# Late gathers with landing places of their own, and a copy on ScalarE

## The chip, the cores and the metric

The kernel runs on one core of one Trainium2 chip. The metric is the device time of one execution in microseconds. TensorE (PE), VectorE (DVE), ScalarE (ACT), GpSimd (POOL) and SyncE (SP) each run an instruction stream of their own and wait for one another through semaphores. SP, ACT and POOL can start DMA transfers.

## The reference

A graph has 6,250 nodes with 64 features each (x), and 200,000 edges sorted by destination, each with a source, a destination, a weight and 64 attributes. Five graph operators are computed and mixed:

```
deg_w = max(segment_sum(w, dst), 1);  deg_c = max(segment_sum(1, dst), 1)
xs    = x[src]
gcn   = segment_sum(w / sqrt(deg_w[src] * deg_w[dst]) * xs) @ Wgcn + b
sage  = x @ Wsage_s + segment_sum(xs) / deg_c @ Wsage_n + b
gin   = ((1 + eps) * x + segment_sum(w * xs)) @ Wgin + b
gconv = x @ Wgc1 + segment_sum(w * xs) @ Wgc2 + b
eop   = segment_sum(w * relu(xs + edge_attr)) @ Wedge + b
out   = layernorm(x + sum of the five, each times its weight)
```

All of it is float32. What costs time is xs = x[src], 200,000 rows of 64 numbers, and the five segment sums.

## The kernel before, in words

The edges are cut into 196 chunks of 1,024 (128 partitions by TILES = 8). A chunk's edges have destinations in a window of at most 40 nodes, so its segment sums are a matrix product: `segment_sums` (L1261) multiplies, for each of the 8 tiles, 128 feature columns (64 of relu(xs + attr), 64 of xs) with 120 columns of one-hot windows (plain, times w, times w and the source's root). Float32 matmuls stand in the profile as two each, so a chunk's product is 16 matmuls of 120 columns. VectorE adds the product to the running sums (`add_sums`, L1065).

The rows of x reach a chunk in three ways:

- 16 **early** chunks: POOL gathers their rows of x at the start (L526), and a chain of ScalarE (L661), TensorE (L1312) and VectorE (L1089 to L1103) finds their root weights.
- 20 **picked** chunks: without DMA. ScalarE makes one-hot nodes (`hot_nodes`, L688 and L691), TensorE multiplies them with the table in SBUF (`pick_tile`, L1280, 14 matmuls of 455 columns per tile of 128 edges), and VectorE picks the row (`pick`, L988 and L992).
- 160 **late** chunks: POOL gathers rows of 68 numbers (64 of x, the inverse root of the degree, padding) from the table `node_table` in DRAM, with 8 indirect DMAs of 128 rows for each chunk (L559).

A late chunk goes round a ring of UNROLL = 4 places, u = 0 to 3. In order of the data:

- ScalarE copies the indices of two chunks, for the next round, into `idx` (L653, semaphore `staged`), when it comes to its own chunk with odd u and the gathers of this pair have landed.
- POOL waits for `staged` and for `chunk_product`, the product of the chunk four before, and gathers into columns D to BLOCK of `feat[:, u]`, the tile that this product reads (L556 to L559).
- VectorE (`features`) waits for `chunk_product`, makes the windows (L1070), waits for the gather, multiplies the root weights (L950) and adds the rows to the attributes (L953, semaphore `summed_in`), which SP has loaded (L421).
- ScalarE (`late_chunk`, L650 to L655) waits for `summed_in` and writes the relu beside the rows (semaphore `relu_ready`).
- VectorE weights the windows (`weigh_hots`, L1076); TensorE (`late_chunk`) waits for relu, windows and the sums of four chunks before, and makes the product.

The stages: a start (degrees, table) with the early gathers; a node stage (L1223, L1228 on TensorE, L627, L635 on ScalarE), during which the first four late chunks are gathered, since `chunk_product` got its start value of 4 when TensorE began; an **early stage** of 4 rounds, in which each late chunk goes with an early one; a **turn stage** of 35 rounds, in which each late chunk goes with one pick tile (two in every seventh) and two half chunks of picked edges go with each seven; one plain round; the end. Every engine runs its instructions in the order written; each loop body is one turn of 28 late chunks. `relu_ready` and its like get their start values on ScalarE behind the node stage (L639). ScalarE's `hot_nodes` stands ahead of its late chunk in four of seven slots.

`window` (L834 to L839) computes the windows of all edges by way of `scratch`, once per pass; there is one pass here.

Of the kernel before, what the change touches and what calls it, by code (L numbers as in the profile page):

```python
# [28 lines left out]
ALU = mybir.AluOpType  # L29
# [56 lines left out]
def build(nc, x, src, dst, edge_attr, edge_weight, mix, Wgcn, bgcn, Wsage_s, Wsage_n, bsage,  # L86
          gin_eps, Wgin, bgin, Wgc1, Wgc2, bgc, Wedge, bedge, out):
    ctx = ExitStack()
    with ctx:
# [26 lines left out]
        row_w = area[:, 4 * CHUNK:6 * CHUNK].rearrange("p (g e) -> p g e", g=2)  # L116

        attr = sb("attr", [P, UNROLL, TILES, D])
        FEATS, HOTS = UNROLL * TILES * BLOCK, UNROLL * TILES * 3 * WINDOW
        ring = sb("ring", [P, FEATS + HOTS])  # L120
        feat = ring[:, 0:FEATS].rearrange("p (u j b) -> p u j b", u=UNROLL, b=BLOCK)

        hot = ring[:, FEATS:FEATS + HOTS].rearrange("p (u j k n) -> p u j k n", u=UNROLL, k=3, n=WINDOW)
        attr_flat = attr[:, :, :, :].rearrange("p u j b -> p (u j b)")
# [13 lines left out]
        e_win = sb("e_win", [P, CHUNKS, TILES], BF16)  # L138

        scratch = sb("scratch", [P, CHUNKS * TILES])  # L140
        e_tmp = scratch[:, :].rearrange("p (c j) -> p c j", j=TILES)
        e_w = sb("e_w", [P, CHUNKS, TILES])

# [158 lines left out]
        hots_ready = sem("hots_ready")  # L302
        summed_in = sem("summed_in")
        relu_ready = sem("relu_ready")
        chunk_product = sem("chunk_product")
        early_idx_loaded, early_gathered = sem("early_idx_loaded"), sem("early_gathered")

# [195 lines left out]
        @block.gpsimd  # L503
        def _(pool):
            nc.gpsimd.memset(ident[:], 0.0).then_inc(pool_chain, 1)
            nc.gpsimd.memset(row_far[:], 0.0).then_inc(pool_chain, 1)
            nc.gpsimd.memset(ones[:], 1.0).then_inc(consts, 1)
            pool.wait_ge(pool_chain, 2)
            nc.gpsimd.affine_select(out=ident[:], in_=ident[:], compare_op=ALU.not_equal, fill=1.0, base=0,
                                    pattern=[[-1, P]], channel_multiplier=1).then_inc(consts, 1)  # L510

            nc.gpsimd.affine_select(out=row_far[:, 0:LAST_OLD], in_=row_far[:, 0:LAST_OLD], compare_op=ALU.not_equal,
                                    fill=FAR, base=-(HIGH - 1), pattern=[[0, LAST_OLD]],
                                    channel_multiplier=1).then_inc(far_ready, 1)
            nc.gpsimd.iota(iota_b[:], [[1, NT]], base=0, channel_multiplier=0,
                           allow_small_or_imprecise_dtypes=True).then_inc(consts, 1)
            nc.gpsimd.iota(minus_ids[:], [[-1, SPLIT]], base=0, channel_multiplier=-SPLIT,
                           allow_small_or_imprecise_dtypes=True).then_inc(consts, 1)
            for t, step, n in ((slots, 1, WINDOW), (cuts, 1, WINDOW + 1), (row_starts, NT, P + 2)):
                nc.gpsimd.iota(t, [[step, n]], base=0, channel_multiplier=0,  # L520
                               allow_small_or_imprecise_dtypes=True).then_inc(consts, 1)

            pool.wait_ge(early_idx_loaded, 16)
            def gather_early(c):
                for j in range(TILES):
                    nc.gpsimd.indirect_dma_start(  # L526
                        out=early_x[:, c, j], out_offset=None, in_=x,
                        in_offset=bass.IndirectOffsetOnAxis(ap=early_idx[:, c, j:j + 1], axis=0),
                    ).then_inc(early_gathered, 16)

            for c in range(HEAD):
                gather_early(c)
                if c == 0:
                    nc.gpsimd.iota(root_part[:, NT:NT + 1], [[0, 1]], base=0, channel_multiplier=1,
                                   allow_small_or_imprecise_dtypes=True).then_inc(consts, 1)
                    nc.gpsimd.iota(minus_mid[:], [[0, 1]], base=-(NT // 2), channel_multiplier=-NT,
                                   allow_small_or_imprecise_dtypes=True).then_inc(consts, 1)

                    nc.gpsimd.memset(table_sb[:, :, D:TROW], 0.0).then_inc(pad_x, 1)
                    nc.gpsimd.memset(table_sb[:, N % NT:, 0:D], 0.0).then_inc(pad_x, 1)  # L540

            pool.wait_ge(base_stored, 1)
            n_pass = pool.value_load(passes[0:1, 0:1], min_val=1, max_val=WINDOWS)
            with pool.Fori(0, n_pass) as v:
                pool.wait_ge(product_g, v * UNITS + 2)
                pool.sem_inc(gathers_begun, 1)
                for c in range(HEAD, EARLY):
                    if c > PACED:
                        pool.wait_ge(weight_done, 2 * (c - PACED) - 1)
                    gather_early(c)  # L550
                pool.wait_ge(table_stored, 16)
                with pool.Fori(0, LATE_STEPS) as i:
                    for u in range(UNROLL):
                        it = v * LATE + i * UNROLL + u
                        pool.wait_ge(staged, v * (LATE // 2) + i * (UNROLL // 2) + u // 2 + 1)
                        pool.wait_ge(chunk_product, it + 1)  # L556
                        pool.sem_inc(gathers_begun, 1)
                        for j in range(TILES):
                            nc.gpsimd.indirect_dma_start(  # L559
                                out=feat[:, u, j, D:BLOCK], out_offset=None, in_=table,  # L560
                                in_offset=bass.IndirectOffsetOnAxis(ap=idx[:, u, j:j + 1], axis=0),
                            ).then_inc(gathered[u], 16)

        @block.scalar
        def _(act):
# [71 lines left out]
                    lift_x(k + 2)  # L637

            act.sem_inc(relu_ready, UNROLL)  # L639
            act.sem_inc(early_relu_ready, 1)  # L640
            act.sem_inc(distance_ready, 1)
            act.sem_inc(relu_g, 2)
# [3 lines left out]
            with act.Fori(0, n_pass) as v:  # L646
                act.wait_ge(early_gathered, early_landed(v))

                def late_chunk(i, u):
                    if u % 2:  # L650
                        act.wait_ge(gathered[u - 1], (v * LATE_STEPS + i + 1) * (16 * TILES))
                        act.wait_ge(gathered[u], (v * LATE_STEPS + i + 1) * (16 * TILES))
                        nc.scalar.copy(idx[:, u - 1:u + 1], e_src[:, bass.ds((i + 1) * UNROLL + u - 1 + BASE, 2)]).then_inc(staged, 1)  # L653
                    act.wait_ge(summed_in, v * LATE + i * UNROLL + u + 1)
                    nc.scalar.activation(feat[:, u, :, 0:D], attr[:, u], ACT.Relu).then_inc(relu_ready, 1)  # L655

                def far_sources(c):
# [82 lines left out]
        def _(dve):  # L740
# [192 lines left out]
            link(nc.vector.memset(win_off[:], 0.0))  # L933
            with dve.Fori(0, n_pass) as v:
                dve.wait_ge(early_gathered, early_landed(v))
                window(v, 0)
                nc.vector.tensor_copy(w_late[:, UNROLL - 1], e_w[:, BASE])

                def features(i, u, last=False):
# [4 lines left out]
                    if u == 1:  # L944
# [2 lines left out]
                        nc.vector.tensor_copy(w_late[:, 0:n], e_w[:, bass.ds(c, n)])  # L947
                    window_hots(hot[:, u], e_win[:, c])
                    dve.wait_ge(gathered[u], turn * (16 * TILES))
                    nc.vector.tensor_tensor(out=wroot[:, u], in0=e_w[:, c], in1=feat[:, u, :, 2 * D], op=ALU.mult)  # L950
                    loaded = (v * (LATE_STEPS + 1) if u > 1 else v * LATE_STEPS) + i + 1
                    dve.wait_ge(attr_loaded[u // 2], (loaded + (u > 1 and last)) * 16)
                    nc.vector.tensor_tensor(out=attr[:, u], in0=attr[:, u], in1=feat[:, u, :, D:2 * D],  # L953
                                            op=ALU.add).then_inc(summed_in, 1)

                def weigh_hots(i, u):
# [409 lines left out]
```

## Time and profile before

| | |
|---|---|
| three runs | 2224.48, 2230.78, 2244.31 us, median 2230.78 |
| the profiled execution | 2228.75 us, its span 2226.9 us |
| TensorE matmul, weight load | 1556.4 us (70%), 1007.5 us (45%) |
| VectorE | 928.6 us (42%) |
| ScalarE | 826.9 us (37%) |
| POOL | 1355.2 us (61%) |
| late gathers, L559 | 1280 instructions, 1228.4 us |
| mean granted TensorE clock | 0.867 of full speed |

Busy time is that of instructions in execution. A matmul's end is modelled. Waits are the idle time of an engine ahead of an instruction, put down to what ended last by the profile; "remote" means that no recorded event explains the end of a wait, "issue" that the engine waited for nothing the profile shows.

### The profile page before, as it was taken

The numbers are of one execution on the slowest core, as the hardware profiler recorded it, in microseconds if no ns is written. First come the engines' busy times: TensorE is split into PE (matmuls) and PEld (weight loads), VectorE is DVE, ScalarE is ACT, GpSimd is POOL, SyncE is SP. The second block draws the span as 40 slices with busy tenths as digits, with TensorE's granted clock in tenths as the row PEclk, the third lists the DMA queues.
The fourth block names the chain that finished last, engine by engine and source line by source line (L and its number), as shares of the span: only waits on it lengthen the run. The fifth ranks groups of instructions, "written<-read, shape, count | busy, mean of one in ns | idle before, by whom it ended". The sixth has DMA issues, their size and how long they took to land.

```text
span 2226.9 us, 22565 instructions
## 1 busy us (share of the span) xinstructions
PE 1556.4 (70%) x6037; PEld 1007.5 (45%) x6037; DVE 928.6 (42%) x2539; ACT 826.9 (37%) x1201; POOL 1355.2 (61%) x1426
## 2 busy tenths in 40 slices
PE   1004367566888777877878778777887888877876
PEld 1003367553554544544445445444444445544546
DVE  5684256543433332433433433243333334423346
ACT  1676233243433433424244234233333324423323
POOL 7665366556666656656666666566666656665660
PEclk9999967688989888978889888888888888888988
DMA  5111234331222222222222222222222222222223
GB/s 98 23 24 51 70 100 112 95 80 42 51 64 45 55 54 46 57 46 44 54 57 53 47 57 43 47 58 50 48 66 43 48 51 57 47 53 44 59 55 77
DMA packets 83186, 126.12 MB, mean 57 GB/s; under 512 B 29494, under 2 KB 31269, under 8 KB 82821
## 3 DMA queue, kind: packets, MB, share of 16 engines
q0 software_dynamic: 45056, 48.85, 13.6%
q1 hardware_dynamic: 36371, 74.90, 11.0%
q10 hardware_dynamic: 1650, 1.04, 0.2%
q8 instruction: 53, 0.87, 0.2%
q14 instruction: 56, 0.46, 0.1%
HBM read 121.29 MB, written 3.40 MB: 56 GB/s over the span
## 4 chain that ended last, share of the span: by engine, by line
PE 43%; issue 18%; another core or an unknown queue 17%; DVE 10%; ACT 4%; POOL 3%; DVEq 2%; DMA 1%; SPq 0%; POOLq 0%; ACTq 0%
PE psum L1280 27%; PE psum L1261 13%; ACT ring L604 4%; POOL ring L559 3%; DVE ring L1076 2%; DVE sums L1065 2%; DVE early L988 1%; PE psum L1312 1%; PE psum L1228 1%; DVE attr L953 1%; DVE early L992 1%; DMA ring<-node_table,idx 1%; PE psum L1341 1%; PE psum L1342 1%
## 5 line engine op out<-in xcount | busy, mean ns | idle before, releaser
L559 POOL DMA_INDIRECT ring<-node_table,idx x1280 | 1228.4, 960 | 758.2 <-issue 389.4
L1280 PE MATMUL psum<-table_sb,early_x 128*128 128x455 f32 x2240 | 988.1, 586 | 115.6 <-issue 110.1
L1280 PEld LDWEIGHTS psum<-table_sb,early_x 128*128 128x128 f32 x2240 | 446.0, 205 | 573.4 <-issue 566.7
L1261 PE MATMUL psum<-ring 128*128 128x120 f32 x2560 | 405.3, 313 | 246.5 <-issue 127.5
L1261 PEld LDWEIGHTS psum<-ring 128*128 128x128 f32 x2560 | 375.5, 224 | 310.2 <-issue 164.9
L988 DVE TENSOR_TENSOR early<-psum,digit_hot 128x455 f32<-128x455 f32 x160 | 100.6, 631 | 989.5 <-remote 599.3
L688 ACT ACTIVATE early_x<-early,minus_ids 128x256 f32<-128x256 f16 x560 | 370.4, 744 | 138.7 <-remote 103.4
L655 ACT ACTIVATE ring<-attr 128x512 f32<-128x512 f32 x160 | 100.2, 626 | 483.4 <-DVE attr L953 383.8
L679 ACT ACTIVATE early<-early 128x256 f32<-128x256 f32 x40 | 16.7, 416 | 518.2 <-DVE early L1009 385.1
L1065 DVE TENSOR_TENSOR sums<-sums,psum 64x40 f32 (+1 forms) x648 | 127.5, 197 | 97.4 <-remote 53.6
L526 POOL DMA_INDIRECT early_x<-in_x,early_idx x128 | 122.0, 953 | 61.4 <-issue 40.3
L1261 PE MATMUL psum<-early 128*128 128x120 f32 x576 | 102.7, 340 | 77.8 <-issue 53.7
L1076 DVE TENSOR_TENSOR ring<-ring,psum 128x320 f32<-128x320 f32 x320 | 141.6, 484 | 6.0 <-issue 1.0
L691 ACT ACTIVATE early_x<-early_x,ones 128x1792 f32<-128x1792 f32 x80 | 143.1, 1788 | 2.6
L1261 PEld LDWEIGHTS psum<-early 128*128 128x128 f32 x576 | 98.0, 251 | 98.5 <-issue 72.7
L953 DVE TENSOR_TENSOR attr<-attr,ring 128x512 f32<-128x512 f32 x160 | 109.6, 685 | 0.0
L877 DVE SCALAR_TENSOR_TENSOR early<-attr,scratch,psum 128x1024 bf16<-128x1024 f32 x80 | 98.1, 1275 | 24.2 <-issue 22.6
L992 DVE TENSOR_REDUCE early<-early 128x65 f32<-128x455 f32 x160 | 98.5, 627 | 4.2
L1236 PE MATMUL psum<-ring 128*128 128x98 f32 (+1 forms) x8 | 2.0, 435 | 137.8 <-DVE ring L894 137.8
L604 ACT ACTIVATE ring<-attr,scratch 128x1024 bf16<-128x1024 f32 x82 | 93.0, 1137 | 10.6 <-issue 10.4
L1070 DVE TENSOR_TENSOR ring<-e_win,psum 128x320 f32<-128x320 f32 (+1 forms) x160 | 77.1, 482 | 18.2 <-issue 11.4
L1236 PEld LDWEIGHTS psum<-ring 128*128 128x128 f32 (+1 forms) x8 | 1.8, 327 | 138.0 <-DVE ring L894 138.0
(158 smaller groups left out, 644.8 us busy)
## 6 DMA issues: line engine op xcount, KB each, us to landing
attr<-in_edge_attr SPq DMA_DIRECT2D x79, 512.0 KB
ring<-node_table,idx POOLq DMA_INDIRECT x1280
early<-in_edge_attr SPq DMA_DIRECT2D x36, 256.0 KB
src_all<-in_src SPq DMA_DIRECT2D x16, 512.0 KB
early<-key_rows SPq DMA_DIRECT2D x10, 512.0 KB
early_x<-degree_rows SPq DMA_DIRECT2D x2, 1568.0 KB
early_x<-in_x,early_idx POOLq DMA_INDIRECT x128
node_table<-table_sb SPq DMA_DIRECT2D x1, 1666.0 KB, 6.0
```

The source lines that it names most:

```text
L526: nc.gpsimd.indirect_dma_start(out=early_x[:, c, j], out_offset=None, in_=x, in_offset=bass.IndirectOffsetOnAxis(ap=early_idx[:, c, j:j + ...
L559: nc.gpsimd.indirect_dma_start(out=feat[:, u, j, D:BLOCK], out_offset=None, in_=table, in_offset=bass.IndirectOffsetOnAxis(ap=idx[:, u, j: ...
L604: last = nc.scalar.activation(signs[0:rows, k % TURNS], row_dst[0:rows, g], ACT.Sign, bias=cuts[0:rows, n:n + 1], scale=-1.0, accum_out=si ...
L688: last = nc.scalar.activation(to[:, :, a], keys[:, tile:tile + 2], ACT.Square, bias=minus_ids[:, a:a + 1])
L691: nc.scalar.activation(to, to, ACT.Relu, bias=ones[:, 0:1], scale=-2.0).then_inc(node_hot_made, 1)
L953: nc.vector.tensor_tensor(out=attr[:, u], in0=attr[:, u], in1=feat[:, u, :, D:2 * D], op=ALU.add).then_inc(summed_in, 1)
L988: nc.vector.tensor_tensor(out=picks[:, k % 2], in0=pick_ps[k % 2].rearrange("p (b c) -> p c b", b=SPLIT), in1=hot_c, op=ALU.mult).then_inc ...
L992: last = nc.vector.tensor_reduce(out=feat_g[:, half, k, D:2 * D + 1], in_=picks[:, k % 2], axis=AX.X, op=ALU.add)
L1065: last = nc.vector.tensor_tensor(out=sums[of, k, to], in0=sums[of, k, to], in1=acc[ps, part * WINDOW:(part + 1) * WINDOW], op=ALU.add)
L1076: return nc.vector.tensor_tensor(out=to[:, :, k], in0=to[:, :, 0], in1=by.unsqueeze(2).to_broadcast([P, n, WINDOW]), op=ALU.mult)
L1261: last = nc.tensor.matmul(to[:, 0:3 * WINDOW], features[:, j, 0:2 * D], hots[:, j].rearrange("p k n -> p (k n)"), start=(j == 0), stop=(j ...
L1280: last = nc.tensor.matmul(pick_ps[k % 2].rearrange("p (b c) -> p b c", b=SPLIT), node_hot[:, k, a], table_sb[:, a * SPLIT:(a + 1) * SPLIT, ...
```

## The change

Late gathers land in four places of their own, `landing`, two of them new and two inside `scratch`. ScalarE copies the 64 features of a landed chunk into the product's tile and increments `lifted`. POOL waits for `lifted` of the chunk four before, not for its product. `lifted` gets its start value of 4 on ScalarE behind the node stage. The product's tile has 128 columns in place of 132. VectorE reads rows and root weight from the landing place. Since two places lie in `scratch`, VectorE's `window` waits for the lifts of the pass before, and POOL waits for `windows_set` ahead of the third chunk of each round (u = 2).

```diff
-        FEATS, HOTS = UNROLL * TILES * BLOCK, UNROLL * TILES * 3 * WINDOW
+        FEATS, HOTS = UNROLL * TILES * 2 * D, UNROLL * TILES * 3 * WINDOW
...
-        feat = ring[:, 0:FEATS].rearrange("p (u j b) -> p u j b", u=UNROLL, b=BLOCK)
+        feat = ring[:, 0:FEATS].rearrange("p (u j b) -> p u j b", u=UNROLL, b=2 * D)
...
+        landing_free = sb("landing", [P, UNROLL // 2, TILES, TROW])
+        landing = [landing_free[:, k] for k in range(UNROLL // 2)] + [
+            scratch[:, k * TILES * TROW:(k + 1) * TILES * TROW].rearrange("p (j b) -> p j b", b=TROW) for k in range(UNROLL - UNROLL // 2)]
...
+        lifted = sem("lifted")
...
 (POOL)
-                        pool.wait_ge(chunk_product, it + 1)
+                        pool.wait_ge(lifted, it + 1)
+                        if u == UNROLL // 2:
+                            pool.wait_ge(windows_set, v + 1)
                         pool.sem_inc(gathers_begun, 1)
                         for j in range(TILES):
                             nc.gpsimd.indirect_dma_start(
-                                out=feat[:, u, j, D:BLOCK], out_offset=None, in_=table,
+                                out=landing[u][:, j], out_offset=None, in_=table,
...
 (ScalarE, behind the node stage)
             act.sem_inc(relu_ready, UNROLL)
+            act.sem_inc(lifted, UNROLL)
...
 (ScalarE, late_chunk)
                     act.wait_ge(summed_in, v * LATE + i * UNROLL + u + 1)
+                    nc.scalar.copy(feat[:, u, :, D:2 * D], landing[u][:, :, 0:D]).then_inc(lifted, 1)
                     nc.scalar.activation(feat[:, u, :, 0:D], attr[:, u], ACT.Relu).then_inc(relu_ready, 1)
...
 (VectorE, ahead of window)
                 dve.wait_ge(early_gathered, early_landed(v))
+                dve.wait_ge(lifted, v * LATE + UNROLL)
...
 (VectorE, features)
-                    nc.vector.tensor_tensor(out=wroot[:, u], in0=e_w[:, c], in1=feat[:, u, :, 2 * D], op=ALU.mult)
+                    nc.vector.tensor_tensor(out=wroot[:, u], in0=e_w[:, c], in1=landing[u][:, :, D], op=ALU.mult)
...
-                    nc.vector.tensor_tensor(out=attr[:, u], in0=attr[:, u], in1=feat[:, u, :, D:2 * D],
+                    nc.vector.tensor_tensor(out=attr[:, u], in0=attr[:, u], in1=landing[u][:, :, 0:D],
```

## Rows read from the trace of the kernel before

**Rows 1.** Page: engines' busy time and share, then the chain by engine.
```profile
PE 1556.4 (70%) x6037; PEld 1007.5 (45%) x6037; DVE 928.6 (42%) x2539; ACT 826.9 (37%) x1201; POOL 1355.2 (61%) x1426
...
PE 43%; issue 18%; another core or an unknown queue 17%; DVE 10%; ACT 4%; POOL 3%; DVEq 2%; DMA 1%; SPq 0%; POOLq 0%; ACTq 0%
```
**Rows 2.** Line L559's instructions: what they waited for, who waited for them.
```profile
  remote: 215.8, 69
  ACT idx L653: 117.4, 18
  PE psum L1261: 35.6, 13
...
  ACT idx L653: 8.3, 1
  DVE psum L950: 5.5, 1
```
**Rows 3.** Timeline: start, duration, instruction, [idle before <- releaser], of three engines.
```profile
1666.39 0.63 ACT L655 ACTIVATE ring<-attr 128x512 f32<-128x512 f32 x1 [2.25 <-DVE attr L953]
...
1677.73 0.94 POOL L559 DMA_INDIRECT ring<-node_table,idx  x1 [2.26 <-remote]
1714.64 1.08 POOL L559 DMA_INDIRECT ring<-node_table,idx  x1 [6.70 <-ACT idx L653]
...
1714.22 0.68 DVE L953 TENSOR_TENSOR attr<-attr,ring 128x512 f32<-128x512 f32 x1
```
**Rows 4.** Windows: start:end, length, busy PE, PEld, DVE, ACT, POOL, clock, DMA share, GB/s.
```profile
718.80:733.80 15.00, 15.00 (x56) 9.37 (x56) 9.78 (x31) 8.02 (x12) 11.32 (x12) 0.91 0.27 67
733.80:740.60 6.80, 1.40 (x8) 0.99 (x6) 0.00 (x0) 0.00 (x0) 3.78 (x4) 0.86 0.23 51
...
780.90:797.90 17.00, 4.79 (x23) 3.56 (x22) 0.00 (x0) 0.00 (x0) 11.44 (x13) 0.66 0.20 35
...
1692.70:1709.70 17.00, 8.96 (x14) 2.83 (x15) 0.00 (x0) 0.00 (x0) 11.58 (x13) 0.75 0.18 27
1714.60:1729.60 15.00, 13.19 (x56) 9.66 (x57) 8.43 (x26) 10.67 (x15) 10.49 (x11) 0.76 0.27 59
```
**Rows 5.** Windows over the node stage.
```profile
197.00:217.00 20.00, 19.55 (x94) 18.02 (x94) 3.65 (x8) 6.53 (x14) 9.43 (x10) 1.00 0.32 104
217.00:232.00 15.00, 3.12 (x14) 2.30 (x12) 0.00 (x0) 0.70 (x2) 11.32 (x12) 1.00 0.19 28
...
247.00:257.00 10.00, 6.93 (x34) 6.37 (x32) 1.00 (x3) 3.15 (x9) 0.00 (x0) 1.00 0.00 0
```
**Rows 6.** POOL's timeline in the early stage.
```profile
285.89 0.94 POOL L559 DMA_INDIRECT ring<-node_table,idx  x1 [2.46 <-remote]
```
**Rows 7.** Windows: the early and the turn stage.
```profile
265.00:480.00 215.00, 139.16 (x786) 134.29 (x787) 125.78 (x361) 72.48 (x88) 125.26 (x128) 0.71 0.38 104
480.00:2140.00 1660.00, 1313.50 (x4693) 784.54 (x4691) 606.88 (x1775) 593.99 (x861) 1049.78 (x1096) 0.87 0.23 51
```
**Rows 8.** POOL's timeline in the turn stage: two bursts begin.
```profile
718.82 0.94 POOL L559 DMA_INDIRECT ring<-node_table,idx  x1 [3.51 <-remote]
...
742.34 0.94 POOL L559 DMA_INDIRECT ring<-node_table,idx  x1 [3.85 <-remote]
```
**Rows 9.** ScalarE's timeline: the node stage's copies, the first relu.
```profile
201.76 0.37 ACT L635 COPY parts_h<-psum 128x256 f32<-128x256 f32 x1 [1.33 <-PE psum L1228]
...
211.57 0.37 ACT L635 COPY parts_h<-psum 128x256 f32<-128x256 f32 x1 [1.02 <-PE psum L1228]
...
256.93 0.64 ACT L635 COPY parts_h<-psum 128x256 f32<-128x256 f32 x2 [1.29 <-PE psum L1228]
...
266.31 0.63 ACT L655 ACTIVATE ring<-attr 128x512 f32<-128x512 f32 x1 [1.84 <-DVE attr L953]
```
**Rows 10.** ScalarE's nearest copy; TensorE's wait for the windows (us, times, longest).
```profile
L670 ACT COPY early<-early_x 128x512 f32 x12 | 7.4, 615 | 23.2 <-issue 10.4 <-PE psum L1261 9.5 <-remote 3.3
...
PE psum L1261 <- DVE ring L1076: 105.3, 32, 7.3
```

## The prediction

> **What bounds the kernel now.** I began with the page's totals [rows 1]. TensorE is busy for 70% of the span, POOL 61%, VectorE 42%, ScalarE 37%, and the chain is 43% TensorE with 18% "issue" and 17% "unknown". A third of the chain is time that no engine owns, so the question is who makes TensorE slow.
>
> Second, the waits around the late gathers [rows 2]. POOL pauses before 100 of its gathers: 69 times "remote" (215.8 us) and 13 times on TensorE's product (35.6 us), 18 times on the copy of indices (117.4 us). The code has only two waits in front of a chunk, `staged` and `chunk_product`, so "remote" is a product whose end the profile doesn't show. 160 chunks over 100 pauses are 1.6 chunks in one uninterrupted burst. The same answer says who waits for a gather to land: 8.3 us once, 5.5 us once, in the whole run. Rows that landed lie there: the gathers that begin at 1677.73 have all been issued 10 us later, and VectorE adds them at 1714.22 [rows 3]. **Gathers are early already**; starting them earlier has 14 us to win, at most.
>
> Third, stretches of single bursts [rows 4], the view on which all rests. I cut five bursts into their first 15 us and what is left of them with some 3 us beyond. In the first 15 us TensorE retires 56 matmuls in the first and 56 in the last of the five, 284 in 75 us in all: 3.8 a us. In the rest it retires 8 in 6.8 us, 10 in 6.6 us (not shown), 23 in 17 us and 14 in 17 us: 55 in 47.4 us, 1.16 a us, and neither VectorE nor ScalarE runs anything. After the next pause it is at full rate again. Call this the crawl.
>
> Is it the gathers? Two other places say so. In the node stage gathers 0 to 3 run without a pause for 40 us [rows 5]: TensorE retires 94 matmuls in the 20 us to 217, then 14 in 15 us, and 34 in the 10 us after the burst, in straight-line code with other operands. And in the early stage POOL runs single chunks (16 in 215 us, 13.4 us each [rows 7]) with pauses like the 2.46 us of [rows 6]: no crawl there. The granted clock doesn't explain it: in the node stage it is 1.00 throughout, in the crawls of rows 4 it is 0.86, 0.66 and 0.75, while the rate falls to a third. By "TensorE: Matmul & The Clock Gate" (The HAM clock gate) of the Trainium skill the array is either at 2.4 or at 1.2 GHz, which could halve the rate and no more; the trace goes beyond it, so the cause must lie elsewhere. The page also reports a clock stuck at a quarter, which would be rival A below.
>
> So POOL and TensorE regulate each other: a long burst makes TensorE crawl, its product comes late, **the product's wait stops POOL, and the stop frees TensorE**.
>
> **The law in numbers.** A burst of n chunks lasts 10n us (12 gathers in 15 us [rows 4], 8 to a chunk). TensorE is at full rate from 3 us after its end to 15 us into the next: p + 12 us, with p the pause. It crawls for 10n − 12 us. A chunk needs 4693 / 137 = 34.3 matmuls (1096 gathers are 137 chunks [rows 7]). So 34.3n = 3.8(p + 12) + 1.16(10n − 12), p = (22.7n − 31.7) / 3.8.
> - n = 2: p = 3.6, 23.6 us, 11.8 a chunk. The trace: bursts of two begin at 718.82 and 742.34 [rows 8], 23.5 apart; the whole stage 1660 / 137 = 12.1.
> - n = 3: p = 9.6, 13.2 a chunk. n = 4: p = 15.6, 13.9 a chunk.
> - n = 1 has no crawl; POOL's 10 us and a pause rule.
>
> **The change, part by part.**
> 1. *The wait on the product becomes a wait on the lift.* ScalarE lifts chunk m before its relu, which precedes the product; the product has a pick tile before it, and in a crawl its own matmuls too. Of the two waits only `staged` and the lift are left. Of 100 pauses the 82 of "remote" and product lose their cause. Rows 3 show one: the gathers of chunk 119 wait 2.26 us for a product, up to 1677.73, though chunk 115's relu was at 1666.39; with the lift they follow at once, and bursts of one and three chunks become one of four. What ends a burst then is the index copy, for which POOL waited 6.70 us up to 1714.64; it is made when ScalarE gets to its odd chunk, which needs VectorE, which needs the pick tiles. I take n = 3, between today's 1.6 and the four places: (13.2 − 12.1) × 137 = **+151 us**. Bounds: n = 2, 11.8 a chunk, −41 us (nothing to +0 if today's mean stays); n = 4, +247 us.
> 2. *The first four chunks.* `lifted` gets its start value on ScalarE behind the node stage, `chunk_product` got it at TensorE's start. So gathers 0 to 3 leave the node stage, and its crawl goes. Copies L635 came every 2.45 us (201.76 to 211.57); the 13th would come at 201.76 + 12 × 2.45 = 231.2 and came at 256.93 [rows 9]: **−26 us**.
> 3. *The same gathers land on the early stage.* The first begins at about 231.5 and its chunk has landed at about 243.5 (10 us of issue and an estimated 2 to land); chunk 0's relu, at 266.31 now [rows 9], would be due at 240.3 and comes at about 244.3: +4 us. POOL goes on through chunk 5, 60 us: 48 us of crawl give 56 matmuls; a chunk of this stage takes 786 / 16 = 49, so 1.1 chunks instead of 48 / 13.4 = 3.6: 2.5 × 13.4 = +33 us. The other ten, in bursts of two: 98 = 3.95(p + 12) + 1.16 × 8 (3.95: 786 in 199 us of work), p = 10.5, 15.2 a chunk against 13.4 [rows 7]: +18 us. Together **+55 us**; bounds 0 (the bursts stay single) and +90.
> 4. *The lift's own cost.* 160 copies of 128x512. Nearest row: L670, the same shape, 615 ns [rows 10]: 98 us on an engine that is idle 63% of the time. On the path it lies where TensorE waits for a relu or hots at the head of a product: 32 waits on L1076 [rows 10] and a few on L655. There the hots end beside the relu, so half of 0.62 × 35 = 22 counts: **+10 us**, bounds 0 and +22. Queued behind it on ScalarE are the relu, the node hots (L688) for the next tiles, and the staging copy.
> 5. *Nothing:* VectorE reads the rows and the root weight from the landing place instead of the block, same shapes. `windows_set` is awaited before the third chunk; the window is two VectorE instructions of 128x1568, about 2 us each as three times L953's 0.68 [rows 3], and two chunks (20 us) of gathers cover it; without that cover it would cost POOL these 4 us, once. VectorE's new wait for the lift's start value moves the window by no more than the first relu's wait for rows (item 3) hides. SP's queue has no new step. The product reads blocks of 128 floats, not 132: no row prices it; 0, bounds ±5.
>
> The sum is made against the profiled execution's own 2228.75 us (span 2226.9), 2 us under the median of 2230.78: 2228.75 + 151 − 26 + 55 + 10 = 2419, with 2 us to the median 2421. I say **2420 us**.
>
> **Rivals.**
> - *A: the crawl is TensorE's own (a clock held low), not the gathers'.* Then landed rows are not awaited anyway, the node stage keeps its crawl, and only the lift is added: 2231 + 10 = 2240. For it: the granted clock does dip in the turn stage. Against it: the node stage at clock 1.00 and the ends of crawls, each within 3 us of a burst's end.
> - *B: POOL's waits are the bound.* The usual rule, "double-buffer for performance" (Trainium Kernel Development and Optimization, Best Practices, in the Trainium skill), would have it so; rows 2 disagree, with 14 us of waiting for landed rows. If the 251 us of pauses for products went and TensorE kept its 3.8 a us (34.3 matmuls in 9.0 us), POOL's 10 us a chunk would pace it: 2231 − 251 + 10 = 1990; with half of that gain 2110. It decides if a burst of three no longer brings a crawl.
> - *C: the staging copies alone hold bursts at two.* Item 1 is 0 instead of +151, item 3 half: 2231 − 26 + 27 + 10 = 2242.
> - *D: as C, and the early stage stays single and the lift is hidden:* 2231 − 26 = 2205.
> - *E: the change doesn't bring gathers forward* because `staged` always comes last: that is C or D in its times.
>
> **Chances.** Forecast 0.64 (2280 to 2600), A 0.07, B 0.14, C with E 0.10, D 0.05. One per cent (22 us) is about what a measurement of this kernel can tell from no change; the three runs lie within 0.9%. Faster by over 1%: B and D, 0.19. Within 1%: A and C, 0.17. Slower: 0.64. The range leaves out B and the uppermost bursts of four: 2200 to 2520; the forecast's own is 2300 to 2520.
>
> **What would show it.** POOL's pauses fall from 100 to 40 to 60, those left mostly on L653. Windows set as in rows 4, from 15 us into a burst to its end, hold about 1.2 matmuls a us and make up over 40% of the turn stage. The first late gather starts near 231 and the last L635 near 231. L655 stands behind an equal copy of 0.62 us. The time between bursts of three is about 40 us. I am wrong if TensorE goes on at 3.8 a us past the 20th us of a burst, or if most pauses stay.

## The result and the profile after

| | before | after |
|---|---|---|
| runs, us | 2224.48 to 2244.31, median 2230.31 (4) | 2482.02 to 2509.45, median 2498.45 (4) |
| the profiled execution, its span | 2228.75, 2226.9 | 2509.45, 2507.6 |
| TensorE's mean granted clock | 0.867 | 0.798 |

The ratio is 1.119, 95% interval 1.112 to 1.126: 268 us slower at the median, where 190 were forecast. 2498 lies inside the range of 2200 to 2520, near its upper end. The profiled execution of after is the slowest of its four, so its stages add up to 281 us and not 268.

The page's totals of after, engines and then the chain, answer to [rows 1]. The matmuls are as many as before; ScalarE has 160 instructions more.

```profile
PE 1626.3 (65%) x6037; PEld 1006.5 (40%) x6037; DVE 927.0 (37%) x2539; ACT 910.8 (36%) x1361; POOL 1349.4 (54%) x1426
...
PE 45%; issue 24%; another core or an unknown queue 15%; DVE 11%; ACT 1%; DVEq 1%; DMA 1%; POOL 1%; SPq 0%; ACTq 0%; POOLq 0%
```

The late gathers of after (L565), what they waited for and who waited for their landing, answer to [rows 2]. The product is gone from the list. POOL waits for the lift (L662) 32 times and for the index copy (L660) 28 times, 601 us together, where its waits were 369 us before ("issue" left out in both). Hardly anybody waits for landed rows, as before: 14.8 us in the whole run.

```profile
  ACT ring L662: 391.3, 32
  ACT idx L660: 210.0, 28
...
  DVE psum L959: 8.6, 2
  ACT idx L660: 6.2, 1
```

Windows over one burst of four chunks in the turn stage of after, then over the start of the next burst of three and its rest, answer to [rows 4] (start:end, length, busy PE, PEld, DVE, ACT, POOL with counts, clock, DMA share, GB/s). TensorE retires 64 matmuls in the first 15 us and 13 in the 28 us after them, up to 3 us past the burst's end; then 61 and 9.

```profile
965.40:980.40 15.00, 13.39 (x64) 8.79 (x64) 7.97 (x23) 11.22 (x17) 11.65 (x12) 1.00 0.25 62
980.40:1008.40 28.00, 9.63 (x13) 3.07 (x12) 1.27 (x4) 4.92 (x8) 18.90 (x20) 0.59 0.22 45
1028.30:1043.30 15.00, 12.18 (x61) 8.03 (x59) 4.42 (x13) 7.67 (x12) 11.34 (x13) 1.00 0.25 62
1043.30:1061.00 17.70, 7.92 (x9) 2.30 (x8) 1.40 (x3) 0.00 (x0) 11.31 (x12) 0.51 0.14 26
```

POOL's timeline, the first gathers of these two bursts. The second one waited 22.91 us for the lift of a chunk whose rows had landed long before. All four places were full, because TensorE had got through only 13 matmuls while they were being filled; during this pause it catches up.

```profile
965.37 1.29 POOL L565 DMA_INDIRECT landing<-node_table,idx  x1 [4.79 <-ACT idx L660]
...
1028.30 0.94 POOL L565 DMA_INDIRECT landing<-node_table,idx  x1 [22.91 <-ACT ring L662]
```

TensorE inside the crawl: two matmuls, each with the weight load behind it (L1289 is the pick tile; the lines of PE's and PEld's timelines are put together in order of time). A matmul of this tile starts every 0.38 us at full rate (14 of them take 5.52 us from 1015.70) and every 2.1 to 2.9 us here, and the starts of these four stand 0.70, 1.40 and 0.70 us apart. The time before each is "issue", which is no wait for another engine that the profile shows.

```profile
992.62 0.92 PE L1289 MATMUL psum<-table_sb,early_x 128*128 128x455 f32 x1 [1.92 <-issue]
993.32 0.29 PEld L1289 LDWEIGHTS psum<-table_sb,early_x 128*128 128x128 f32 x1 [1.80 <-issue]
...
994.72 0.92 PE L1289 MATMUL psum<-table_sb,early_x 128*128 128x455 f32 x1 [1.18 <-issue]
995.42 0.29 PEld L1289 LDWEIGHTS psum<-table_sb,early_x 128*128 128x128 f32 x1 [1.81 <-issue]
```

The node stage of after, windows, then ScalarE's timeline with its last copy and the first relu, answer to [rows 5] and [rows 9]. The stage keeps its 4.7 to 4.9 matmuls a us to the end, and the gathers begin behind it (at 228.42).

```profile
197.00:217.00 20.00, 20.00 (x98) 18.60 (x97) 2.94 (x6) 8.19 (x17) 0.00 (x0) 1.00 0.22 89
217.00:228.00 11.00, 10.47 (x52) 9.95 (x51) 0.63 (x3) 3.97 (x10) 0.00 (x0) 1.00 0.01 1
```
```profile
227.08 0.64 ACT L641 COPY parts_h<-psum 128x256 f32<-128x256 f32 x2 [1.29 <-PE psum L1237]
...
241.60 0.62 ACT L663 ACTIVATE ring<-attr 128x512 f32<-128x512 f32 x1
```

**Where the time went.** I cut both executions at the relus of late chunks 0, 16 and 156. Up to the first: 266.3 before, 241.6 after, −24.7. The sixteen chunks of the early stage: 208.7 and 281.2, +72.4. The 140 chunks up to number 156: 1681.4 and 1923.4, 12.0 and 13.7 us each, +242.0. The end: 70.4 and 61.4, −9.0, which no item of the forecast has and no run explains. The sum is 280.7, the difference of the spans (all differences are of unrounded times). Counted as matmuls of one product or pick tile that stand more than 1.15 us apart, joined to stretches, TensorE crawls for some 320 us before, in 56 stretches, and for some 790 us after, in 51: about as many stretches, nearly three times as long. (How they are joined matters: the gaps inside the tiles alone make 311 and 672 us.)

A second count needs no threshold for a slow matmul. Take of each burst in those 140 chunks what lies behind its first 15 us. Before, these pieces make 398 us (24%) with 1.8 matmuls a us; after, 617 us (32%) with 0.76. Outside them TensorE retires 3.2 and 3.3 a us, in 1284 and 1307 us. So 219 of the 242 us lie in the long ends of bursts.

### The profile page after: what moved, and what is told of

Its sections match the earlier page's. It is cut to its first block, busy times and chain, and to the rows that moved or that the text cites. A ratio compares the mean times of both kernels' runs of the same rounds, so it can differ in the third digit from the quotient of the medians.

```text
span 2507.6 us, 22767 instructions
## 1 busy us (share of the span) xinstructions
PE 1626.3 (65%) x6037; PEld 1006.5 (40%) x6037; DVE 927.0 (37%) x2539; ACT 910.8 (36%) x1361; POOL 1349.4 (54%) x1426
## 4 chain that ended last, share of the span: by engine, by line
PE 45%; issue 24%; another core or an unknown queue 15%; DVE 11%; ACT 1%; DVEq 1%; DMA 1%; POOL 1%; SPq 0%; ACTq 0%; POOLq 0%
PE psum L1289 30%; PE psum L1270 12%; DVE early L885 3%; DVE ring L1085 1%; PE psum L1321 1%; DVE sums L1074 1%; DVE early L997 1%; PE psum L1237 1%; ACT early_x L696 1%; DVE attr L962 1%; POOL landing L565 1%; PE psum L1350 0%; PE psum L1351 0%; PE psum L1232 0%
## 5 line engine op out<-in xcount | busy, mean ns | idle before, releaser
L1289 PE MATMUL psum<-table_sb,early_x 128*128 128x455 f32 x2240 | 1072.6, 615 | 297.9 <-issue 297.3
L565 POOL DMA_INDIRECT landing<-node_table,idx x640 | 612.4, 957 | 550.6 <-ACT ring L662 227.4
L565 POOL DMA_INDIRECT scratch<-node_table,idx x640 | 610.3, 954 | 492.0 <-issue 204.6
L1289 PEld LDWEIGHTS psum<-table_sb,early_x 128*128 128x128 f32 x2240 | 460.6, 211 | 826.9 <-issue 826.3
L1270 PE MATMUL psum<-ring 128*128 128x120 f32 x2560 | 396.3, 301 | 285.2 <-issue 194.4
L1270 PEld LDWEIGHTS psum<-ring 128*128 128x128 f32 x2560 | 361.5, 214 | 352.3 <-issue 253.9
L662 ACT COPY ring<-scratch 128x512 f32<-128x512 f32 x80 | 49.1, 614 | 480.5 <-DVE attr L962 423.9
L662 ACT COPY ring<-landing 128x512 f32<-128x512 f32 x80 | 49.1, 613 | 271.8 <-DVE attr L962 217.5
L1270 PE MATMUL psum<-early 128*128 128x120 f32 x576 | 94.4, 325 | 44.8 <-issue 22.1
L1270 PEld LDWEIGHTS psum<-early 128*128 128x128 f32 x576 | 91.4, 238 | 64.7 <-issue 39.9
## 6 DMA issues: line engine op xcount, KB each, us to landing
early_x<-degree_rows SPq DMA_DIRECT2D x2, 1568.0 KB, 13.7
```

Source lines behind the costliest of these rows:

```text
L565: nc.gpsimd.indirect_dma_start(out=landing[u][:, j], out_offset=None, in_=table, in_offset=bass.IndirectOffsetOnAxis(ap=idx[:, u, j:j + 1] ...
L1270: last = nc.tensor.matmul(to[:, 0:3 * WINDOW], features[:, j, 0:2 * D], hots[:, j].rearrange("p k n -> p (k n)"), start=(j == 0), stop=(j ...
L1289: last = nc.tensor.matmul(pick_ps[k % 2].rearrange("p (b c) -> p b c", b=SPLIT), node_hot[:, k, a], table_sb[:, a * SPLIT:(a + 1) * SPLIT, ...
```

## The experiments

Each was timed beside the kernel before on the same chip. That kernel takes 2205 us on the first of the three chips used, 2229 on the second, so ratios are compared (the changed kernel's is 1.119). Unless said otherwise an experiment is the changed kernel with one edit.

**Was it the freed gathers, or the lift?** `product_wait` puts the old wait back and leaves all else.

```diff
                         pool.wait_ge(lifted, it + 1)
+                        pool.wait_ge(chunk_product, it + 1)
```

> The changed kernel with the old wait on chunk_product put back ahead of each late chunk, beside the wait on the lift: the lift, its copies, the landing places and the later start stay, the freedom of the gathers goes. Crawl theory: bursts go back to those of the kernel before, 2231 - 30 (node stage) + 20 (first gathers on the early stage) + 10 (lift) = 2230 us, range 2210 to 2270. Rival 'the lift and the new tiles cost the time': stays near 2500.

2207.84 us against 2205.22: ratio 1.004 (1.001 to 1.008). The loss is gone with one wait, though the lift, its 160 copies and the landing places are all still there.

`late_start` is the kernel before with only the later start:

```diff
                 pool.wait_ge(table_stored, 16)
+                pool.wait_ge(relu_ready, UNROLL)
```

> The kernel before, only POOL waits for the end of ScalarE's node stage ahead of the first late gather. Crawl theory: node stage -30 (no gathers beside it), the first four chunks then run unpaused beside the early stage, +20: 2220 us, range 2200 to 2240. What product_wait takes beyond this is the lift's own cost, expected 10 us, 0 to 22. Rival 'the node stage is slow of itself': no -30, 2250 or more.

2208.95 us, ratio 1.001 (0.996 to 1.005). In its profile the node stage ends 32 us earlier (last copy at 225.4, before 257.4), and chunk 16's relu comes at 483.3 where it came at 475.0: the gathers' crawl is paid once, beside the one stage or the other. Against product_wait this leaves −1 us for the lift. Each of the two was run ten times and spreads over 33 us, so this can't be told from some 10 us either way.

**Do pauses end the crawl?** `pause8` and `pause16` make POOL wait for the landing of its own last gather.

```diff
                             ).then_inc(gathered[u], 16)
+                            if j == TILES - 1:               # pause16: and u % 2 == 1
+                                pool.wait_ge(gathered[u], (v * LATE_STEPS + i) * (16 * TILES) + 16 * (j + 1))
```

> The changed kernel, and POOL waits after each late chunk for the landing of its own last gather before it issues the next chunk. Crawl theory (gathers issued without a pause for some 15 us make TensorE crawl, a pause of 2 to 3 us ends it): bursts are 10 us, no crawl, POOL's 9.7 + 2.9 = 12.6 us a chunk rules: turn stage 137 x 12.6 = 1726 against 1660 before (+66), node stage -30, early stage 16 x 12.6 = 202 against 215 (-13): about 2255 us, 240 us faster than the changed kernel although POOL does the same work and waits more. Rival 'TensorE's own clock': nothing changes, about 2500. Rival 'it is the lift or the new tiles that cost': nothing changes or slower by the added waits, 2500 or more.

> The changed kernel, and POOL waits for the landing of its last gather after every second late chunk. Crawl theory: bursts of 20 us with some 5 us of crawl and a pause of 2.9: 22.3 us for two chunks if TensorE gets its 68.6 matmuls in: 3.8 x 17.3 + 1.16 x 5 = 71.5, just enough: 11.2 to 11.6 us a chunk, turn stage 1530 to 1590, sum 2070 to 2150 us: faster than both kernels. If the crawl's rate is 0.5 a us and its onset at 13 us, TensorE falls behind and bursts stretch as before, about 2200. Rival 'TensorE's own clock': 2500.

2287.25 us (ratio 1.038, 1.030 to 1.045) and 2400.37 (1.091, 1.083 to 1.099). With a pause behind each chunk there is no stretch of crawl in the whole run, and the kernel with more waits takes 7% less time than the changed one, by the ratios. POOL's timeline in pause8, the first gathers of two chunks, and the windows over these two chunks: the chunk before ended 2.4 us earlier, the chunks begin 12.2 us apart, and TensorE retires 32 and 44 matmuls. That pace, 12.4 us in the mean, is what the kernel now takes.

```profile
705.39 0.94 POOL L565 DMA_INDIRECT landing<-node_table,idx  x1 [2.42 <-DMA landing<-node_table,idx]
...
717.60 0.95 POOL L565 DMA_INDIRECT scratch<-node_table,idx  x1 [2.52 <-ACT idx L662]
```
```profile
705.40:717.60 12.20, 10.70 (x32) 7.08 (x33) 3.97 (x13) 7.79 (x12) 7.55 (x8) 0.72 0.15 24
717.60:729.80 12.20, 12.16 (x44) 6.58 (x42) 5.79 (x18) 1.40 (x3) 7.57 (x8) 1.00 0.34 87
```

With a pause behind each second chunk TensorE crawls for some 490 us in 76 stretches. The 2070 to 2150 expected for it were wrong: 20 us of gathers with 2.6 us behind them still bring the crawl. `pause13` (the loop goes over two rounds, with a pause behind every 13th gather) asks where the limit is:

> The changed kernel, and POOL waits for the landing of its last gather after every 13th (five pauses in 64 gathers), ahead of the point where the crawl sets in. Crawl theory: (80 + 5 x 2.6) / 8 = 11.6 us a chunk, little crawl: 240 + 205 + 140 x 11.6 + 65 = 2135 us, up to 2200: between 0 and 3% faster than the kernel before, and 5% faster than pause8 and pause16. If the onset were a matter of chunks or of POOL's loop and not of gathers in a row, it would lie between pause8 and pause16, 2287 to 2400.

2302.74 us, 1.032 (1.028 to 1.036): a miss, against 2135 to 2200. It crawls in 60 stretches, some 335 us. Of the 44 bursts of 12 gathers and more in its turn stage that begin behind a pause under 2.5 us (mostly 2.3), 26 retire only 13 to 30 matmuls of products and picks in their first 15 us. Of the 26 behind a longer pause one does; the others retire 41 to 66. So a pause of 2.3 us often does not undo 16 us of gathers, while 2.4 us undo 10. The expectation's other branch, an onset set by chunks or by POOL's loop, named a place between pause8 and pause16; the ratio is no higher than pause8's 1.038, which speaks against it, but the intervals overlap. No setting of pauses tried beats the kernel before.

**What in the gathers is it?** `narrow` fetches 16 bytes for each late row in place of 272, so its output is not the right one; `landing_free` is cleared once at the start:

```diff
-                                out=landing[u][:, j], out_offset=None, in_=table,
+                                out=landing[u][:, j, 0:4], out_offset=None, in_=table.rearrange("n (k w) -> (n k) w", w=4),
```

> The changed kernel, whose late gathers fetch pieces of 4 numbers (16 bytes) in place of rows of 68 (272 bytes), as many descriptors and as many gathers (the numbers fetched are others). If bytes moved by the gathers cause the crawl, it shrinks or goes: 2000 to 2250 us. If the issue of gathers or the descriptors cause it, nothing changes: 2450 to 2520 us.

2493.21 us, 1.119 (1.110 to 1.129): the changed kernel's time with a seventeenth of the bytes in a late row, and with a seventh of all the bytes of the gathers' queue, early gathers included (its line in narrow's page, then in after's: packets, MB, share).

```profile
q0 software_dynamic: 45056, 6.91, 4.6%
```
```profile
q0 software_dynamic: 45056, 48.85, 11.2%
```

Windows over a burst in narrow show 68 matmuls in 15 us and 11 in the 26 us after them.

```profile
762.30:777.30 15.00, 14.51 (x68) 9.22 (x66) 7.57 (x21) 10.23 (x15) 11.34 (x13) 1.00 0.15 35
777.30:803.70 26.40, 9.25 (x11) 3.06 (x11) 0.00 (x0) 3.26 (x5) 17.87 (x19) 0.59 0.11 21
```

`memset7` keeps POOL busy with an eighth of the DMAs. Seven of eight rows are zeros in it, so its output is not the right one either; the waits of ScalarE and VectorE for landed rows are fitted to one gather and the memsets (not shown):

```diff
-                        for j in range(TILES):
-                            nc.gpsimd.indirect_dma_start(...).then_inc(gathered[u], 16)
+                        nc.gpsimd.indirect_dma_start(...)        # j = 0 alone
+                        for j in range(2 * (TILES - 1)):
+                            nc.gpsimd.memset(landing[u][:, 1:TILES], 0.0).then_inc(filler, 1)
+                            pool.wait_ge(filler, it * (2 * (TILES - 1)) + j + 1)
```

> The changed kernel, in which seven of the eight gathers of each late chunk are left out: in their place POOL runs 14 memsets of 128x476 on the landing place, about as long as the gathers were (seven eighths of the rows are zeros). POOL stays as busy, only the indirect DMAs are gone. If the gathers themselves make TensorE crawl: no crawl, POOL's 10 us a chunk or TensorE's 9.0 rules, 240 + 180 + 140 x 10.3 + 65 = 1930 us, up to 2050. If any unbroken work of POOL's makes it crawl: about 2500. If it is TensorE's own clock: about 2500 too.

2042.95 us, 0.917 (0.915 to 0.920), and no stretch of crawl. POOL's timeline, the end of one chunk and the gather of the next; then windows over two chunks, which take 10.9 and 11.0 us.

```profile
607.04 0.49 POOL L571 MEMSET landing<- 128x476 f32 x1 [0.15 <-POOL landing L571]
607.69 0.49 POOL L571 MEMSET landing<- 128x476 f32 x1 [0.15 <-POOL landing L571]
609.28 0.95 POOL L566 DMA_INDIRECT scratch<-node_table,idx  x1 [1.10 <-issue]
```
```profile
554.10:565.00 10.90, 9.47 (x28) 6.43 (x29) 3.85 (x12) 7.60 (x12) 7.90 (x15) 0.69 0.18 51
565.00:576.00 11.00, 11.00 (x47) 6.81 (x46) 3.74 (x11) 7.61 (x11) 7.91 (x16) 1.00 0.15 53
```

`busy_pause` puts five memsets of 128x544 ahead of each chunk's gathers, each waited for:

```diff
+                        for k in range(5):
+                            nc.gpsimd.memset(landing[u], 0.0).then_inc(filler, 1)
+                            pool.wait_ge(filler, it * 5 + k + 1)
...
                         for j in range(TILES):
```

> The changed kernel, with five memsets of 128x544 by POOL (about 3 us) ahead of the gathers of each late chunk: a pause in the gathers, but none in POOL's work. If a pause in the gathers is enough to end the crawl: no crawl, 9.7 + 3.2 = 12.9 us a chunk, 240 + 206 + 140 x 12.9 + 65 = 2320 us. If POOL has to stand still: crawls as in the changed kernel and POOL's extra 3 us a chunk, 2500 to 2700 us.

2519.78 us, 1.131 (1.128 to 1.135). The time alone looks like a failure of the theory that a pause ends the crawl; the profile says the opposite. There is no stretch of crawl: TensorE retires 33 and 41 matmuls in two chunks of 14 us each. POOL's timeline shows 4.2 us between the gathers, not 3.2, and a chunk takes 14.0 us, by POOL alone:

```profile
611.24 0.94 POOL L571 DMA_INDIRECT scratch<-node_table,idx  x1 [0.30 <-issue]
612.18 0.57 POOL L567 MEMSET scratch<- 128x544 f32 x1
...
616.36 0.95 POOL L571 DMA_INDIRECT scratch<-node_table,idx  x1 [0.79 <-POOL scratch L567]
```
```profile
573.00:587.00 14.00, 7.83 (x33) 4.63 (x32) 6.83 (x22) 2.30 (x5) 10.46 (x13) 0.89 0.31 76
587.00:601.00 14.00, 10.22 (x41) 7.26 (x41) 3.87 (x12) 6.92 (x10) 10.43 (x14) 0.87 0.13 20
```

So the crawl stays away though POOL itself works on; only the price for the memsets was 1 us too low. What pause8 and busy_pause don't tell is whether it is the pause that does it, or the slower pace of gathers that comes with it.

**Is it the pace, or the pause?** `spaced4` and `spaced3` put a memset of one column behind every second (about every third) gather. POOL waits for them only once, ahead of the next chunk:

```diff
+                        pool.wait_ge(filler, it * 4)         # spaced3: it * 3
...
+                            if j in (1, 3, 5, 7):            # spaced3: (2, 4, 7)
+                                nc.gpsimd.memset(spare[:, u * TILES + j:u * TILES + j + 1], 0.0).then_inc(filler, 1)
```

> The changed kernel with a one-column memset on POOL behind every second gather, so that the gathers come at 1.55 us each on average (12.4 us a chunk) and never pause for more than about 1.1 us. Pace theory (the crawl comes when gathers run at more than about one per 1.5 us for some 15 us: pause8 had 1.51 us each and no crawl, pause13 1.42 us each and crawls): no crawl, 240 + 205 + 140 x 12.4 + 65 = 2245 us, like pause8. Pause theory (only 2 us and more without a gather end or prevent it): crawls in long stretches, 2500 us or more.

> The same with three memsets a chunk: 1.48 us a gather, 11.8 us a chunk. Pace theory: at the edge; without crawl 240 + 195 + 140 x 11.8 + 65 = 2150 us, 3% faster than the kernel before; with some crawl, as pause13, 2200 to 2300. Pause theory: 2500.

2503.44 us, 1.134 (1.124 to 1.143), and 2485.93, 1.128 (1.120 to 1.136). They don't tell: the memset fell into the 0.30 us that stood between two gathers anyway, so the pace hardly changed, and TensorE crawls for about 600 us in both. POOL's timeline in spaced4:

```profile
908.01 0.94 POOL L569 DMA_INDIRECT landing<-node_table,idx  x1 [0.30 <-issue]
908.94 0.13 POOL L574 MEMSET spare<- 128x1 bf16 x1
909.26 0.95 POOL L569 DMA_INDIRECT landing<-node_table,idx  x1 [0.19 <-issue]
```

`waited4` and `waited3` have a wait behind each memset instead (`pool.wait_ge(filler, ...)`), which keeps the next gather back:

> As spaced4, whose memsets fell into the 0.30 us between two gathers and left them 1.28 us apart, but POOL now waits for each memset before it issues the next gather: by the 0.79 to 1.10 us seen between a waited-for memset and a gather in the two kernels with memsets, 1.55 to 1.7 us a gather, 12.5 to 13.7 us a chunk, no gap above 1.3 us. Pace theory: no crawl, 240 + 210 + 140 x 13 + 65 = 2335 us (2265 to 2435). Pause theory (only about 2 us and more without a gather prevent it): crawls as in spaced4 (500 us and more of them), 2500 us or more.

> The same with three waited-for memsets a chunk: 1.48 to 1.6 us a gather, 11.9 to 12.8 us a chunk. Pace theory: little crawl (pause8 had none at 1.51 us a gather in the mean, pause13 some at 1.42), 240 + 195 + 140 x 12.3 + 65 = 2220 us (2165 to 2300). Pause theory: 2480 us, as spaced3.

2298.44 and 2203.02 us, no crawl in either. That reads like the pace theory, but they ran on the third chip, and the kernel before shows that they prove nothing: **the kernel before took 1831.39 us there** (7 runs, 1829.96 to 1835.66), so the ratios are 1.254 (1.251 to 1.258) and 1.203 (1.200 to 1.205). Nothing in the two traces of this chip crawls. The clearest place is code that none of these kernels touches, at the start, beside the early gathers. VectorE's timeline in the kernel before (a chain of small dependent steps), then in waited4:

```profile
45.69 0.16 DVE L868 SCALAR_TENSOR_TENSOR ring<-ring 128x2 f32<-128x2 f32 x1 [1.23 <-DVE ring L867]
46.39 0.17 DVE L867 TENSOR_SCALAR ring<-ring 128x2 f32<-128x2 f32 x1 [0.54 <-issue]
47.79 0.20 DVE L868 SCALAR_TENSOR_TENSOR ring<-ring 128x2 f32<-128x2 f32 x1 [1.23 <-issue]
```
```profile
38.05 0.16 DVE L883 SCALAR_TENSOR_TENSOR ring<-ring 128x2 f32<-128x2 f32 x1
38.24 0.17 DVE L882 TENSOR_SCALAR ring<-ring 128x2 f32<-128x2 f32 x1
38.45 0.16 DVE L883 SCALAR_TENSOR_TENSOR ring<-ring 128x2 f32<-128x2 f32 x1
```

Windows over the same stretch, before and then waited4: POOL's gathers are as many and stand 1.25 us apart in both, but VectorE and ScalarE are busy for twice and five times as long.

```profile
30.00:60.00 30.00, 3.77 (x20) 2.80 (x18) 14.32 (x47) 5.24 (x6) 22.97 (x24) 1.00 0.26 34
```
```profile
30.00:60.00 30.00, 3.38 (x16) 2.61 (x16) 27.23 (x65) 28.46 (x49) 22.99 (x24) 1.00 0.19 30
```

It is the chip and not the kernel: in this stretch VectorE is busy for 8.8 to 17.3 us in every one of the twelve traces from the other chips, and for 27.2 in both from the third. There is no profile of the kernel before on that chip, and the changed kernel was not run on it; that its 1831 us are 2205 without the crawl is likely and not shown. Whether the change would gain there, as rival B has it, is open, and so is pace against pause on a chip that crawls.

## Why the prediction was right, and where its sizes were off

**The bound.** Right: TensorE's slow stretches beside unbroken gathers. Rival A (TensorE's own clock) is out: pause8 and busy_pause make the stretches vanish by edits of POOL's stream alone, memset7 by taking gathers away, and the slow steps of VectorE above stand in a window whose granted clock is 1.00. Inside after's two crawls shown above the granted clock is 0.59 and 0.51, in the 15 us before each 1.00; the rate falls from 4.3 and 4.1 matmuls a us to 0.5, and half a clock doesn't give an eighth of the rate. The clock records of both traces hold full speed and half of it, and no quarter. Late loading of code, a rival that the prediction doesn't name, doesn't explain the first of these crawls: from 978 to 1020 us no packet of a queue of kind "instruction" moves in after. Rival B (POOL's waits are the bound) is out on the chips that crawl. On the third chip the prediction's law fails, since it gives the kernel before some 2230 us there and 1831 were measured. Rivals C, D and E fell with the turn stage's +242, E also with the 32 waits for the lift.

**Item 1, the turn stage, +151, measured +242.** The sign and the mechanism hold, two sizes did not. The prediction took bursts of three throughout; counting pauses of 1.95 us and more, after has 67 bursts (2.4 chunks each; 88 of 1.8 before): 19 of one chunk, 16 of two, 22 of three, 10 of four and more. By the law that alone would have made the term smaller. The other size is the crawl's rate, 1.16 matmuls a us from four stretches. In after the rest of a burst, up to 3 us past its end, holds 7 to 13 matmuls in 20 of the 22 bursts of three (18 us) and 11 to 23 in the eight of four (28 us): more length brings few more matmuls, and the mean is 0.75 a us. With 10 in place of 1.16 (10n − 12), the law reads p = (34.3n − 10) / 3.8 − 12: 11.7 us a chunk for n = 2, 14.1 for n = 3, 15.4 for n = 4. The measured 13.7 lies between.

That repair is not shown, for neither law holds length by length. From one burst's start to the next, in the turn stage of after, a chunk takes 15.5 us in bursts of one, 14.1 in bursts of two, 12.5 in bursts of three and 15.2 in bursts of four. In the kernel before, seven bursts of three took 12.1 us a chunk, where the law gives 13.2, and bursts of two took 12.1 as well. The prediction tested its law at n = 2 only; these seven bursts were there to test it at n = 3. So the balance within one burst gave the direction; for the size no law is shown. That the term came within a factor of two is in part luck: a burst length too long stood against a rate too high.

**What ends a burst.** The prediction said the index copy. After has 32 waits for the lift (391 us), with all four places full, and 28 for the copy (210 us). In the prediction's count (100 before) these are 60 pauses, at the edge of its 40 to 60; by length, 66 are of 1.95 us and more (87 before) and 76 of 0.5 and more (106 before). Of its other signs, the rest of the bursts, from 15 us on, makes 32% of the turn stage, not over 40, at 0.76 matmuls a us and not 1.2; bursts of three begin 37.6 us before the next burst, not 40; the first gather comes at 228.4 and the last node copy at 227.5 for its 231.

**Items 2 and 3.** Node stage −26: measured −24.7 to the first relu, −30 to the last copies. (The copy at 256.93 is the twelfth and not the thirteenth, which came at 257.35; so counted the item would have been −28 or −26.) Early stage +55: measured +72.4. Its first burst runs for 61 us and from its 15th us to 3 us past its end there are 53 matmuls in 48.8 us, where the prediction had 56 in 48. The first six chunks lose 43 us, where it had 37, and the last ten lose 30 where it had 18, although the bursts of two follow each other at 14.6 us a chunk and not 15.2: ahead of the last of these relus ScalarE waits 19.5 us for a DMA of `key_rows` (up to 515.97), where it waited 8.5 before.

**Item 4, the lift, +10.** Measured −1 us between product_wait and late_start, give or take some 10. L662 takes 614 ns, as L670 did with 615; that it costs nothing on the path is neither shown nor excluded.

**The chances.** The forecast's own range stands in two versions, 2280 to 2600 and 2300 to 2520; 2498 lies in both.

**The point that decided** was the sign of a wait: the pauses for the product looked like 251 us of loss and were what kept TensorE running. product_wait shows it with one line.

## What to carry to other kernels

Before a wait is taken away, look at what the other engines do while it lasts and right after. Windows of equal length, set from the start of a burst, showed TensorE at a quarter of its rate and less, which busy shares and the chain of waits never did. When a law is read from bursts, test it on every burst length that the trace has.

"Double-buffer for performance" (Trainium Kernel Development and Optimization, Best Practices, in the Trainium skill) asks to overlap DMA with compute. The kernel before did so already, and to free the buffers still earlier made it 1.119 times as long: the engine set free slowed the one that mattered, and nobody had been waiting for its data.

And run the kernel before on each chip beside an experiment: what bounds a kernel on one can be absent on the next.

## What the runs showed of the hardware

- Where indirect DMAs of 128 rows are issued by POOL every 1.25 us, TensorE slows down once they have run for 11 to 19 us (30 of the 31 bursts of three chunks and more in after's turn stage). VectorE slows down too: at the start of the kernel before, 18 us after the gather at 20.55. TensorE's instructions (993.32, 994.72, 995.42) and VectorE's small steps (45.69, 46.39, 47.79) then start 0.70 us apart or twice that, where such steps of VectorE's start 0.20 us apart on the third chip. ScalarE ran three instructions without a gap in such a stretch (from 984.12 to 985.35 in after). The slow stretch is over about 3 us after the last gather of a burst.
- It doesn't depend on the bytes of a row (narrow) or on POOL's being busy (memset7, busy_pause). Whether the number of DMAs or the number of rows counts, no run separates. With 8 gathers in a row and 2.4 us without there is none; with 13 and 2.3, or 16 and 2.6, it is back.
- It was seen on two of three chips. The kernel before takes 2205 and 2229 us on those and 1831 on the third, and the third chip's two traces don't have it. What causes it is not known.
- A memset of 0.13 us fits into the 0.30 us between two gathers for nothing. A gather behind a memset that is waited for starts 0.79 us after that memset's end (busy_pause, waited4), in memset7 once 1.10 us.
